# Resident expert weights, in-place states and a new order of the step in a fused attention and mixture-of-experts kernel

## The reference

```python
x = L0_attn_query
xn = _layernorm(x, axis=-1)
x = x + _L0_attn_ref(xn, ...) + _L0_ffn_ref(xn, ...)
...
scores = x_flat @ Wg
topk_scores, topk_idx = jax.lax.top_k(scores, K)
topk_w = jax.nn.softmax(topk_scores, axis=-1)
for e in range(E):
    h = jax.nn.gelu(x_flat @ W1[e] + b1[e], approximate=False)
    out_e = h @ W2[e] + b2[e]
    y = y + cw[:, e:e + 1] * out_e
```

## Time and profile before

| | us |
|---|---|
| runs: lowest, median, highest of 3 | 1478.45, 1484.06, 1485.84 |
| the profiled execution, its own time | 1484.62 |
| span, first to last instruction | 1482.9 |
| TensorE busy (matmul) | 947.4, 64% of the span |
| TensorE busy (weight load) | 750.0, 51% |
| VectorE busy | 578.7, 39% |
| ScalarE busy | 740.2, 50% |
| GpSimd busy | 431.4, 29% |
| mean granted clock of TensorE | 0.813 of full |
| moved by DMA | 210.90 MB, mean 142 GB/s |

### The profile page before, as it was taken

How to read it: one execution, slowest core, us unless ns; L and a number is a source line. 1 busy time by engine, 2 the same in 40 slices (tenths; PEclk the granted TensorE clock), 3 DMA queues, 4 the chain that set the end, 5 groups by cost and what they waited for, 6 DMA issues and landing times.

```text
span 1482.9 us, 28381 instructions
## 1 busy us (share of the span) xinstructions
PE 947.4 (64%) x10529; PEld 750.0 (51%) x10529; DVE 578.7 (39%) x1098; ACT 740.2 (50%) x1602; POOL 431.4 (29%) x389
## 2 busy tenths in 40 slices
PE   3454748487583866858486594848658574866842
PEld 2324547375462746656364464637446463746531
DVE  5541615345160443437152252525425151433421
ACT  3422637365361755727373472836445282655522
POOL 3064101035022130707132040424603021251146
PEclk9865979889796897968798797878978787987965
DMA  7326474755847566695855758485674838576462
GB/s 216 103 82 150 124 148 118 148 158 160 152 135 126 135 146 143 170 173 147 159 133 129 145 149 151 126 178 145 161 159 133 145 106 178 147 151 153 132 103 71
DMA packets 320744, 210.90 MB, mean 142 GB/s; under 512 B 155296, under 2 KB 281952, under 8 KB 320096
## 3 DMA queue, kind: packets, MB, share of 16 engines
q1 hardware_dynamic: 311392, 188.10, 55.9%
q0 software_dynamic: 8192, 16.79, 3.8%
q10 hardware_dynamic: 1024, 4.20, 1.8%
HBM read 147.51 MB, written 61.50 MB: 141 GB/s over the span
## 4 chain that ended last, share of the span: by engine, by line
PE 42%; issue 26%; ACT 17%; POOL 5%; DVE 3%; SPq 3%; DMA 2%; ACTq 1%; POOLq 0%; DVEq 0%
PE ps_h L677 11%; PE ps_f L685 8%; PE ps_a L755 6%; PE ps_r L834 6%; PE ps_k L743 3%; POOL rows_in L1280 3%; ACT hid L1107 2%; PE ps_a L781 2%; ACT L1107 2%; ACT expo L1075 1%; ACT xy L1023 1%; PE ps_f L669 1%; PE ps_f L687 1%; ACT L1075 1%; ACT xy L1045 1%
## 5 line engine op out<-in xcount | busy, mean ns | idle before, releaser
L677 PE MATMUL ps_h<-turned,w_tile 128*128 128x128 f32 x1248 | 216.0, 328 | 334.0 <-issue 235.3
L677 PEld LDWEIGHTS ps_h<-turned,w_tile 128*128 128x128 f32 x1248 | 190.5, 231 | 371.4 <-issue 266.2
L1107 ACT ACTIVATE hid<-ps_h,w_tile 128x128 f32<-128x128 f32 x624 | 178.2, 368 | 340.5 <-PE ps_h L677 336.5
L685 PE MATMUL ps_f<-w_tile,hid 128*128 128x128 f32 x1248 | 198.7, 312 | 0.7 <-ACT turned L1100 0.7
L685 PEld LDWEIGHTS ps_f<-w_tile,hid 128*128 128x128 f32 x1248 | 187.0, 229 | 1.5 <-issue 1.0
L1252 POOL TENSOR_TENSOR sqx<-sqx,sqy 128x512 f32<-128x512 f32 x64 | 82.0, 1303 | 344.4 <-ACT sqy L1031 255.6
L1280 POOL DMA_INDIRECT rows_in<-xn,row_of x128 | 128.3, 1003 | 183.2 <-DVE tile_expert L1637 146.9
L1252 POOL TENSOR_TENSOR v_tok<-qkv,rnorm 128x512 f32<-128x512 f32 x16 | 41.4, 2587 | 395.3 <-DVE rnorm L1533 341.0
L834 PE MATMUL ps_r<-sqx,mats 128*128 128x512 f32 x256 | 132.6, 642 | 17.8 <-POOL sqx L1252 9.6
L1295 POOL DMA_INDIRECT got<-rows_out,row_of x112 | 109.1, 974 | 102.1 <-DMA rows_out<-turned 70.3
L755 PE MATMUL ps_a<-k_rows,q_rows 128*32 128x16 f32 x4096 | 102.2, 245 | 41.6 <-DMA k_rows<-states 29.0
(11 more groups left out here) (249 smaller groups left out, 1566.5 us busy)
## 6 DMA issues: line engine op xcount, KB each, us to landing
w_tile<-w_cat SPq DMA_DIRECT2D x156, 514.0 KB
states<-fxyT SPq DMA_DIRECT2D x32, 512.0 KB, 2.9
k_rows<-states SPq DMA_DIRECT2D x128, 128.0 KB, 5.4
x_tile<-rows_in SPq DMA_DIRECT2D x156, 64.0 KB, 3.1
rows_out<-turned SPq DMA_DIRECT2D x156, 64.0 KB
q_rows<-states SPq DMA_DIRECT2D x128, 64.0 KB, 5.1
rows_in<-v_rows SPq DMA_DIRECT2D x2, 2496.0 KB, 12.0
v_dram<-v_tok SPq DMA_DIRECT2D x16, 256.0 KB, 4.0
```

What stands on the lines that cost most here:

```text
L677: last = nc.tensor.matmul(ps_h[:, c, :], w_tile[:, n % WS, c * P:(c + 1) * P], turned[:, x_turn(n) % FS, 0, :], start=True, stop=True)
L685: nc.tensor.matmul(ps_f[:, 1, :], hid[:, n % 2, c, :], w_tile[:, n % WS, HID + c * C:HID + (c + 1) * C], start=(c == 0), stop=False)
L1107: act.activation(hid[:, n % 2, c, :], ps_h[:, c, :], ACT.Gelu, bias=w_tile[:, n % WS, HID + HC * C + c:HID + HC * C + c + 1]).then_inc(hid ...
```

## The change

- **Weights.** `w_cat`, its three buffers and `load_weights` go. W1, the bias columns b1 and W2 of all 8 experts lie in SBUF (`w_res`), and b2 in `b2_res`. W2 and b2 are read in place with an address from a register: `tile_down` begins with a `value_load` on TensorE. W1 and b1 are copied by VectorE into one of three buffers `w_up`, two tiles ahead (`copy_ups`), with a `value_load` of its own. The group's table is held until TensorE has done its last tile.
- **Room.** `fxyT` goes: depths 1 and 2 and the final states are made in place in `xy1`, and the two turned parts in `xy2`. `x_sb` goes: x is loaded into `xn` and normalised in place. `power`, `below`, `sqp` and `mixed` lie in `u` and `w_rows`. `got` has one buffer in place of two, so a gather waits for the addition before.
- **Stores.** `store_states` and `store_mixed` are issued by ScalarE behind slot 7.
- **Order.** On TensorE the pattern moves behind slot 1 and the target tiles; `grow_once` ahead of slot 3, `turn_w` behind slot 4, `weighted` and `mix_circuits` later. On ScalarE the exponentials move behind `control1`, and the layer norm beside `amplitude`, which uses the same table. On SyncE `load_values` stays at 7, `load_states` moves to 9 and `load_mixed` to 11. On GpSimd a second gather of a step stands behind the first block's `add_rows`.

```diff
-        fxyT = sb("fxyT", [P, 2, 2, BT])
-        w_tile = sb("w_tile", [P, WS, WCOLS])
-        b2_tile = sb("b2_tile", [3, WS, C], BF16)
+        w_res = sb("w_res", [P, E, WCOLS])
+        w_up = sb("w_up", [P, WS, UP])
+        b2_res = sb("b2_res", [3, E, C], BF16)
-        got = sb("got", [P, 2, 2, T, C])
+        got = sb("got", [P, 2, T, C])
...
             def tile_up(n):
                 pe.wait_ge(turn_copied.sem, turn_copied.value(x_turn(n)))
-                pe.wait_ge(w_landed.of(n), w_landed.value(n))
+                pe.wait_ge(up_copied.sem, up_copied.value(n))
...
             def tile_down(n):
+                g, s = n // TILES, n % TILES
...
+                e = pe.value_load(tile_expert[0:1, g % GS, s:s + 1], min_val=0, max_val=E - 1)
                 pe.wait_ge(hidden_ready.sem, hidden_ready.value(n))
                 pe.wait_ge(turn_copied.sem, turn_copied.value(y_turn(n) - 1))
                 for c in range(HC):
-                    nc.tensor.matmul(ps_f[:, 1, :], hid[:, n % 2, c, :], w_tile[:, n % WS, HID + c * C:HID + (c + 1) * C],
-                                     start=(c == 0), stop=False)
+                    w2 = w_res[:, bass.ds(e, 1), UP + c * C:UP + (c + 1) * C].rearrange("p e n -> p (e n)")
+                    nc.tensor.matmul(ps_f[:, 1, :], hid[:, n % 2, c, :], w2, start=(c == 0), stop=False)
...
+            def copy_ups(k, first, last):
+
+                for n in step_tiles.get(k, [])[first:last]:
+                    for m in ((0, 1, 2) if n == 0 else (n + 2,)):
...
+                        e = dve.value_load(tile_expert[0:1, g % GS, s:s + 1], min_val=0, max_val=E - 1)
+                        if m >= WS:
+                            dve.wait_ge(hidden_ready.sem, hidden_ready.value(m - WS))
+                        dve.tensor_copy(w_up[:, m % WS, :], w_res[:, bass.ds(e, 1), 0:UP].rearrange("p e c -> p (e c)")
+                                        ).then_inc(up_copied.sem, 1)
...
+            def store_states(k):
+                if k >= 1:
+                    act.wait_ge(qk_loaded, 16 * 4 * T * k)
+                act.dma_start(states[0:2].rearrange("e p n -> p e n"), xy1[:, :, 0, :]).then_inc(states_stored, 16)
+                act.dma_start(states[2:4].rearrange("e p n -> p e n"), xy1[:, :, 1, :]).then_inc(states_stored, 16)
+                act.wait_ge(turned_k.sem, turned_k.value(k))
+                act.dma_start(states[4], sqy[:, 0, :]).then_inc(states_stored, 16)
...
                 if at >= NB - 2:
-                    pool.wait_ge(proj_psum.sem, proj_psum.value(NB - 1))
-                elif at >= 2:
-                    pool.wait_ge(added_step.sem, added_step.value(at - 2))
+                    pool.wait_ge(xT_psum.sem, xT_psum.value(NB - 1))
+                    pool.wait_ge(scattered[NG - 1], 16 * 2 * GT)
+                elif at >= 1:
+                    pool.wait_ge(added_step.sem, added_step.value(at - 1))
...
-                for b in combined_at.get(k, []):
-                    add_rows(b)
+                for m, b in enumerate(waiting):
+                    if m >= 1:
+                        gather(b)
+                    if b in combined:
+                        add_rows(b)
```

More of the change, by code:

```diff
@@ L60 @@
 ROWS = TILES * P
-WCOLS = HID + HC * C + HC
+UP = HID + HC
+WCOLS = UP + HC * C
 STATES = 5
@@ L244, in build @@
         u = sb("u", [P, 2, 4 * P])
+        power, below = (u[:, 0, n * 2 * P:(n + 1) * 2 * P].rearrange("p (n j) -> p n j", j=NH) for n in range(2))
         signed = [u, expo.rearrange("p c n -> p (c n)").rearrange("p (h n) -> p h n", h=2)]
         sup_mat = sb("sup_mat", [P, 2 * HD])
-        mixed = sb("mixed", [P, 4 * P])
-        scratch = [k_rows.rearrange("p r n -> p (r n)"), fxyT.rearrange("p a g c -> p (a g c)"),
+        scratch = [k_rows.rearrange("p r n -> p (r n)"), xy1.rearrange("p a g c -> p (a g c)"),
                    expo.rearrange("p c n -> p (c n)")]
@@ L324, in build @@
         stored = landing("stored", YS)
-        w_landed = landing("w_landed", WS, 2)
+        up_copied = signal("up_copied")
         rows_landed = landing("rows_landed", XT)
@@ L432, in got_at @@
             if at < NB - 2:
-                return got[:, at % 2]
-            first = (NB - 6) % XN if at == NB - 2 else (NB - 4) % XN
-            return xnT[:, first:first + 2, :].rearrange("p s (t c) -> p s t c", t=T)
+                return got[:]
+            first = 2 * (at - (NB - 2))
+            return xn[:, first:first + 2]
         def mat(name):
@@ L629, in _ @@
                     s = n % TILES
-                    if n == 0:
-                        for m in range(WS):
-                            load_weights(m)
                     if s == 0:
@@ L676, in tile_up @@
                 for c in range(HC):
-                    last = nc.tensor.matmul(ps_h[:, c, :], w_tile[:, n % WS, c * P:(c + 1) * P],
+                    last = nc.tensor.matmul(ps_h[:, c, :], w_up[:, n % WS, c * P:(c + 1) * P],
                                             turned[:, x_turn(n) % FS, 0, :], start=True, stop=True)
@@ L889, in _ @@
                     target_tiles(n)
+                if exists(k):
+                    pattern(k)
                 if exists(o):
@@ L1320, in _ @@
                 o, n = k - 1, k + 1
-                for b in gathered_at.get(k, [])[0:1]:
-                    gather(b)
+                combined = combined_at.get(k, [])
+                waiting = gathered_at.get(k, [])
+                if waiting:
+                    gather(waiting[0])
                 scatter_part(k, 0)
@@ L1327, in _ @@
                     sum_squares(n, sq1_ready, sum1_ready)
-                for b in gathered_at.get(k, [])[1:3]:
-                    gather(b)
                 scatter_part(k, 1)
@@ L1333, in _ @@
                 scatter_part(k, 2)
-                for b in combined_at.get(k, []):
-                    add_rows(b)
+                for m, b in enumerate(waiting):
[3 more added lines that the diff above has]
+                        add_rows(b)
+                for b in combined:
+                    if b not in waiting:
+                        add_rows(b)
                 scatter_part(k, 3)
-                for b in gathered_at.get(k, [])[3:]:
-                    gather(b)
         @block.vector
@@ L1723, in _ @@
                     norm_squares(n)
+                if routed is not None:
+                    route(routed)
+                copy_ups(k, 0, 1)
+                if exists(n) and exists(k):
+                    normalise(n)
+                copy_ups(k, 1, 2)
+                if exists(o):
+                    measure(o)
                 if exists(j):
```

289 lines of the change are left out of this document (132 added, 157 removed).

## The result

| | us |
|---|---|
| after: lowest, median, highest of 4 runs | 1515.91, 1524.60, 1527.58 |
| before, in the same comparison: median of 4 | 1483.05 |
| ratio after to before, 95% interval | 1.0274, 1.0224 to 1.0323 |
| profiled execution after, its span | 1524.91, 1523.2 |
| TensorE, VectorE, ScalarE, GpSimd busy | 988.2, 698.5, 748.7, 433.2 |

The prediction was 1296 us (1225 to 1400), with 0.93 on faster. The time is 229 us above it, and on the other side of no change.

A forecast was written before the change was run, and what follows sets the result against it. TensorE was taken to set the pace, waiting about a sixth of the time, chiefly for tile weights. Eight terms, led by -229 for those waits, summed to -189 from 1484.62, so 1296 us, range 1225 to 1400.

The forecast's parts named there:

- Term 1: TensorE's product into ps_h: all 13 weight waits go, -229, and part of a token-row wait, -12.
- term 2: TensorE's first tile behind each weight wait runs at the full clock: 13 x 2.0, -26.
- Term 3: Register loads on TensorE, one a tile, are hidden: 0, bounds 0 and 179.
- term 4: VectorE's copies of w_up and register loads delay the copy ahead of grown_once: +18, bounds 0 and 182.
- Term 5: ScalarE issuing the stores delays copy_proj and a tile's GELU, for which TensorE waits: +14, bounds 0 to 28.
- term 6: New order: wait ahead of a step's third tile shrinks, -39; token rows behind q/k loads, +21; together -18.
- Terms 7 and 8: One got buffer stops ScalarE and TensorE in steps 5, 9, 13, +45; gathers at the end come later, +19.
- rival D: Long wait was for full DMA engines or q and k; the pattern or another takes it over: 1429, chance 0.05.
- Rival A: Token rows on SyncE's queue take the weights' place and land late in most steps: 1375 us, chance 0.17.
- Rival C: Register loads ahead of every tile_down aren't hidden on TensorE: 1.4 us a tile, 1514 us, chance 0.05.

The follow-up runs named there:

- e5: The kernel before with only the first three weight loads, 153 left out (a pricing run, no usable version): 1358.1 us, ratio to before 0.919.
- e15: e9's memory with the order of before on TensorE, ScalarE and VectorE, q and k loaded right behind v: 1429.9 us, ratio to before 0.966.
- e9: e3 with the states of depth 2 not in place, so turned_states waits for no square: 1390.9 us, ratio to before 0.941.
- e3: The change with a second buffer for gathered rows, gathers issued as before the change: 1465.9 us, ratio to before 0.991.
- e10: e3 with only the first three copies of W1 on VectorE, 153 copies and their register loads left out: 1468.0 us, ratio to before 0.991.
- e17: e15 with only the first three copies of W1 on VectorE: 1443.2 us, ratio to before 0.971.
- e11: e3 with the stores of states and mixed issued by SyncE again: 1495.7 us, ratio to before 1.012.
- e14: e9 with 8 buffers for token rows and with spread and control1 first: 1357.2 us, ratio to before 0.918.

## Why the prediction was wrong

Steps that can be compared one by one, in us:

| from | to | measured | predicted |
|---|---|---|---|
| before | e5: no weight loads | -120 | -267 (terms 1, 2) |
| e5 | e15: resident weights, copies, stores, layer norm in place, places of loads | +70 | +32 (terms 3, 4, 5) |
| e15 | e9: the new order | -37 | -18 (term 6) |
| e9 | e3: states wait for the squares | +73 | no term |
| e3 | after: one got buffer, the end | +55 | +64 (terms 7, 8) |
| sum | | +41 | -189 |

- **Term 1** failed, and term 2 held: in the profiled executions TensorE is idle for 96 us less in e5, where term 1 has 241, and busy for 35 less, where term 2 has 26. The step that failed stands under rival D: "behind the long wait the pattern was held for 1.04 us only (745.57)". I read that as the whole of the pattern's wait for q and k. But `pattern` waits for its loads once, ahead of its first product, at 739.07; a break behind 224 products is no wait for them, and what it is stays open. What the row does show is that nothing was left to wait for at 739.07. The view of DMAs shows when the last load of k_rows had landed:

```profile
L551 SPq DMA_DIRECT2D k_rows<-states x1: 431/431/431, 726.0 to 726.0; - x1
...
DMA to landing us min/median/max: 7.7/7.7/7.7
```

  Issued at 726.03, it landed at 733.7, 1.3 us before the long wait ended (734.96). Take the 17.57 us away and the pattern stands there at 721.5 and waits 12.2 us; the same place of e5 has 12.50. Two waits stood one behind the other for transfers issued in one row on one queue, and the first covered the second. The right form of the term was 17.6 less what the waits behind it grow by. Rival A (token rows, +54) and rival D (+90 at the pattern) were both true at once; I had priced them as alternatives. 238 less 90 and 54 is 94, near the 96.
- **No term for the states in place.** I costed the new waits of VectorE by what they hold on VectorE (term 4), and read "in place" as memory only. With it `turned_states` got its wait for `sq2_ready`, and nothing in my sum asked what ran beside the pair once it waited. The Trainium skill (SBUF — State Buffer, Terms) says that VectorE and GpSimd share one pair of ports to SBUF, held by one of them for a whole instruction. By that rule, as an estimate, two pairs of 2.48 us need 4.96 us when they start together; in after they were through in 4.55 (703.73 to 708.28). The measurement decides: the two get in each other's way as the page says, but by 0.4 us less than one at a time would. The estimate would have shown, ahead of the run, the 2 of the 5 us a step that the slower pair costs.
- **Term 3** held. TensorE's register loads are hidden: its group of w_res waits 3.0 us in all. One load takes

```profile
L644 PEldq TENSOR_LOAD <-tile_expert x156: 296/302/1060, 142.2 to 1425.3; - x156
```

  a median of 302 ns, where I had 462 from SyncE's queue. Rival C did not happen, though the time came out near its 1514; a right number from it would have been luck.
- **Term 4** (+18) was 0 (e10, e17). **Term 5** was priced as a cost of 14, and the wait it named is there: TensorE waits ahead of the projection for 38.6 us in e3 and 23.2 in e11, 15 less. What it left out is what SyncE is spared; with both, ScalarE's stores are a gain of 31 against stores on SyncE (e11).
- **Term 6** had the sign right and gave half the size, 18 where 31 to 37 were measured; its mechanism was right in part, and the rest is luck. From e15 to e9 the wait it named, for a copied turn, fell by 21 us (89.3 to 68.1) where it has 39. More came from the pattern's wait, which fell from 146.3 to 38.0 us, and from that for token rows, 103.6 to 59.1, which the term has rising by 21. Against it the waits rose ahead of the products of sqx (19.2 to 74.9) and of a (3.9 to 48.6).
- **Terms 7 and 8** held: 45 + 19 = 64 against 55 by e3. The three stalls of 20.5, 20.5 and 19.7 us stand where some 4 us are waited for anyway, so 48 for them against 45; at the end the wait for meas is 14 us shorter (30.46 to 16.10), against 19.
- **Open:** 70 us between e5 and e15, of which the copies are none. In the profiled executions TensorE is idle for 50.5 us more in e15: 16.2 ahead of the projection (24.0 to 40.2), the wait that ScalarE's stores make, 14.4 at the pattern and 13.6 at the token rows; and it is busy for 27.6 more. The layer norm in place, the new places of SyncE's loads and the register loads are in it, and none of these was undone in the old order.
- **Signs.** No "issue" wait stood at the product into ps_h, 82 MB less were moved, and ScalarE waited 13.75 us for a gather, as forecast. The granted clock did not rise above 0.85: it was 0.805, and 0.813 before.

The range failed for the same reason as the sum: its upper end came from rivals taken one at a time, and no case joined two of them.

## What to carry to other kernels

Before a wait is booked as gain, look up when the data of the next waiting instruction behind it land. If that is shortly before the first wait ends (here 1.3 us), the second instruction shows no wait in the trace and will take over most of the first one's. When a buffer is dropped to make room, list the waits that the sharing adds and what other engine is released by the same event, for that is what will run beside the delayed instruction. And the largest idle time of an engine with slack is no guide: 162 us taken from VectorE's did not pay for 30 us of later loads, while 5 us a step on the states' chain moved the kernel by 73.

## What was not expected of the hardware

- VectorE's SCALAR_TENSOR_TENSOR on 128 x 1024 floats, all operands in SBUF, took 1277 to 1282 ns (before, e9, e14) and 2296 in after, beside GpSimd's sum of two 128 x 512 pieces, which itself went from 2.48 us a pair to 3.46.
- A register load took 302 ns on TensorE and 305 on VectorE in after, and 462 on SyncE's queue in the kernel before.
- With 81 MB less to move, the DMA share in the wait for q and k was no lower in e5, 1.22, than it was in the long wait before, 1.03. The whole kernel's packets fell only from 320744 to 297783 there: that speaks for the packets and against the bytes as what fills the engines, and was not tried by itself.
